# The middle stage's value products with the values as TensorE's weights, two heads in the two halves of its columns

## The reference, cut to what matters

```python
xn, ln_lat = layer_norm(ctx), layer_norm(x)          # 375 and 112 rows a batch
q = ln_lat @ Wq                                      # 16 heads x 64
k, v = split(concatenate([xn, ln_lat]) @ Wkv)        # 487 rows
weight = softmax(einsum('bhld,bhnd->bhln', q * scale, k * scale), masked)
out = einsum('bhln,bhnd->bhld', weight, v)           # 112 x 64 for each head
x = x + tanh(g) * (out.reshape(b, 112, 1024) @ Wout)
# then layer norm, and a router that picks 2 of 8 experts for each token
```

## Time and profile before

| | |
|---|---|
| median of three runs | 1403.51 us |
| the profiled execution's own time | 1406.79 us |
| its span, first to last instruction | 1405.0 us |
| mean granted TensorE clock | 0.937 |
| TensorE matmul busy | 1225.0 us, 87% |
| VectorE busy | 1083.2 us, 77% |
| ScalarE busy | 999.4 us, 71% |
| GpSimd busy | 813.3 us, 58% |

### The profile page before, as it was taken

One profiled execution on the slowest core, in us unless ns is written; L12 is line 12 of the kernel. 1 busy time (PEld: TensorE's weight loads), 2 busy tenths in 40 slices (PEclk: granted clock), 3 DMA queues, 4 the chain that ended last, 5 costly groups with the idle time before them and its releaser, 6 DMA issues. The chain is left out here.

```text
span 1405.0 us, 38066 instructions
## 1 busy us (share of the span) xinstructions
PE 1225.0 (87%) x13060; PEld 880.3 (63%) x13060; DVE 1083.2 (77%) x3112; ACT 999.4 (71%) x2552; POOL 813.3 (58%) x1204
## 2 busy tenths in 40 slices
PE   3999999999986499999999999999999974489994
PEld 1777777777764245566656566656666653389894
DVE  3799999999985168888888888888888882477872
ACT  2888888888883358877787887787888771256562
POOL 3544444444454346677777777777777674146564
PEclk7799999999987599999999999999999985699997
DMA  5444545455420148877788777878777793854333
GB/s 162 131 146 144 148 120 169 114 151 155 134 50 7 49 94 156 141 147 146 153 158 160 143 146 154 147 151 163 152 144 152 137 196 61 316 154 60 57 36 76
DMA packets 309406, 185.50 MB, mean 132 GB/s; under 512 B 257930, under 2 KB 295186, under 8 KB 306112
## 3 DMA queue, kind: packets, MB, share of 16 engines
q1 hardware_dynamic: 293024, 140.82, 47.3%
q0 software_dynamic: 13168, 35.80, 10.5%
q10 hardware_dynamic: 3024, 6.47, 1.5%
HBM read 76.19 MB, written 49.94 MB: 90 GB/s over the span
## 5 line engine op out<-in xcount | busy, mean ns | idle before, releaser
L1682 ACT ACTIVATE b_prob<-b_prob,b_top 112x487 f32<-112x487 f32 x256 | 178.9, 699 | 28.3 <-DVE b_top L1808 26.5
L1315 POOL TENSOR_TENSOR b_halves<-b_prob,b_halves 112x487 f16<-112x487 f32 x128 | 146.9, 1148 | 83.7 <-ACT b_halves L1707 82.2
L1493 PE MATMUL b_ps_p<-w_s,b_tok_s 128*128 128x512 f16 (+1 forms) x768 | 187.7, 381 | 4.0 <-DVE b_k_s L1795 3.2
L1493 PE MATMUL b_ps_p<-b_tok_s,w_s 128*128 128x487 f16 x768 | 181.9, 374 | 6.6 <-POOL b_tok_s L1309 3.7
L1808 DVE CUSTOM_DVE_ANT_0 b_prob<-b_ps_s,b_keep 112x487 f32<-112x487 f32 x256 | 167.3, 655 | 13.2 <-PE b_ps_s L1586 11.6
L717 ACT ACTIVATE a_prob<-a_prob,a_top 112x375 f32<-112x375 f32 x256 | 154.8, 605 | 3.7 <-DVE a_top L853 2.0
L1707 ACT ACTIVATE b_halves<-b_prob 112x487 f16<-112x487 f32 x256 | 156.0, 609 | 0.6
L853 DVE CUSTOM_DVE_ANT_0 a_prob<-a_ps_s,a_keep 112x375 f32<-112x375 f32 x256 | 138.1, 540 | 21.7 <-PE a_ps_s L610 21.4
L618 PE MATMUL a_ps_t<-a_const,a_prob 112*125 112x112 f32 x768 | 135.7, 287 | 10.6 <-ACT a_prob L717 9.1
L1601 PEld LDWEIGHTS b_ps_o<-b_v_s,b_pT 128*128 128x128 f16 (+1 forms) x3072 | 123.9, 99 | 31.4 <-DMA b_pT<-b_halves 11.6
L1601 PE MATMUL b_ps_o<-b_v_s,b_pT 128*128 128x64 f16 (+1 forms) x3072 | 135.0, 195 | 9.2 <-DMA b_pT<-b_halves 9.1
(11 more groups left out here) (263 smaller groups left out, 3022.9 us busy)
## 6 DMA issues: line engine op xcount, KB each, us to landing
xs<-a_blank SPq DMA_DIRECT2D x14, 1032.0 KB, 4.5
c_w_pool<-w_split SPq DMA_DIRECT2D x8, 1600.0 KB, 10.6
b_wch_f<-in_w_experts POOLq DMA_DIRECT2D x32, 384.0 KB, 5.2
w_split<-b_wch_s POOLq DMA_DIRECT2D x32, 384.0 KB, 3.9
a_k_stack<-keys SPq DMA_DIRECT2D x96, 93.8 KB, 3.1
a_ctx_f<-in_ctxT SPq DMA_DIRECT2D x16, 375.0 KB, 3.8
keys<-a_k_s SPq DMA_DIRECT2D x16, 375.0 KB, 3.2
b_ctx_t<-in_ctx SPq DMA_DIRECT2D x16, 375.0 KB
```

What stands on the lines that cost most here:

```text
L1315: pool.tensor_tensor(halves[:, h % TURN, LO, 0:NK], prob[:, h % RING, 0:NK], halves[:, h % TURN, HI, 0:NK], ALU.subtract).then_inc(s_lo[1], 1)
L1493: last = pe.matmul(out, sta(a, k), mov(m, k), start=(k == 0 and n == 0), stop=(k == tiles - 1 and n == 2))
L1682: act.activation(prob[:, h % RING, 0:NK], prob[:, h % RING, 0:NK], ACT.Exp, bias=top[:, h % RING:h % RING + 1], scale=-1.0, accum_out=sums ...
```

## The change

Values and probabilities change places in `values`. It is called once for a pair of heads, at even steps, six steps behind (`PAIRLAG`). It does 24 matmuls: weights are 64 columns of the values, moving are the 112 columns of `pT`, and the two heads alternate between output partitions 0 to 63 and 64 to 127, each with its half of the array's columns. The output thus stands in `ps_o` with the head's 64 numbers in the partitions and the tokens in the columns, as Wout's product wants it.

Since the softmax sums lie in one partition for each token, they can't scale that output directly. So the reciprocals of eight heads are turned by TensorE (`H_T`, one transpose of 112 x 8), split into high and low by VectorE (`rT`, scaled by 4096), spread over the partitions by TensorE (`H_B`, eight matmuls with weights of 8 rows, `picks`), copied to SBUF by ScalarE (`r_f`) and multiplied with `ps_o` by VectorE (`o_f`). ScalarE takes the high half of `o_f` (`out_high`), GpSimd the low half (`out_low`). `o_n`, its multiplication, the eight transposes a batch and the VectorE low half of `oT` are gone. The "h" parts of a batch are seven, not five, and lie at steps 0, 1, 5, 9, 13, 14, and the first one at step 15 of the batch itself.

```diff
-LAG = 5
+PAIRLAG = 6
-        pT = sb("pT", [128, TURN, 2, NB1, 128], F16)
+        pT = sb("pT", [128, TURN, 2, NB1, T], F16)
-        H_T, H_O, H_X, H_G, HI_ = 0, 2, 3, 4, 5
+        H_T, H_B, H_O, H_X, H_G, NH = (0, 2), (1, 3), 4, 5, 6, 7
+        FREED = (2, 3, 5, 6, 7, 8, 9)
-        XSLOT = {1: ("h", 0), 2: ("r", 0), 3: ("q", 0), 4: ("q", 1), 6: ("h", 1), 8: ("n", 0), 9: ("h", 2), 10: ("n", 1), 11: ("n", 2),
-                 13: ("h", 3), 14: ("h", 4)}
+        XSLOT = {0: ("h", H_B[0]), 1: ("h", H_T[1]), 2: ("r", 0), 3: ("q", 0), 4: ("q", 1), 5: ("h", H_B[1]), 8: ("n", 0), 9: ("h", H_O),
+                 10: ("n", 1), 11: ("n", 2), 13: ("h", H_X), 14: ("h", H_G), 15: ("t", H_T[0])}
 # GpSimd
+            def out_low(c, i):
+                need(pool, s_hhi, AH, c, A_O[i], settled)
+                pool.tensor_tensor(oT[:, LO, 4 * i:4 * i + 4, :], o_f[i][:, :].rearrange("p (j n) -> p j n", j=4), oT[:, HI, 4 * i:4 * i + 4, :],
+                                   ALU.subtract).then_inc(s_olo, 1)
 # GpSimd, body
+                        if s in (3, 7):
+                            out_low(b - 1, s // 7)
 # TensorE, hitem
-                if k < H_O:
-                    for n in range(4):
-                        j = 4 * k + n
-                        last = pe.transpose(ps_x[:, n * T:(n + 1) * T], o_n[:, 2 * j:2 * j + 2, :].rearrange("p h d -> p (h d)"), ident[0:T, 0:T])
+                if k in H_T:
+                    i = H_T.index(k)
+                    need(pe, s_rsum, 2, c, i + 1)
+                    last = pe.transpose(ps_x[0:8, 0:T], rsum[:, 8 * i:8 * i + 8], ident[0:T, 0:T])
+                elif k in H_B:
+                    for j in range(4):
+                        for part in (HI, LO):
+                            last = pe.matmul(ps_x[:, j * T:(j + 1) * T], picks[:, j, :], rT[:, part, :], start=(part == HI), stop=(part == LO))
 # TensorE, values
-                        last = pe.matmul(ps_o[h // 8][:, col:col + D1], pT[0:k, h % TURN, a, j, :],
-                                         v_s[par][0:k, m, j, h * D1:(h + 1) * D1], ...
+                        for half in range(2):
+                            h = 2 * pair + half
+                            last = pe.matmul(ps_o[pair // 4][64 * half:64 * half + 64, cols], v_s[par][0:k, m, j, h * D1:(h + 1) * D1],
+                                             pT[0:k, h % TURN, a, j, :], ...
 # ScalarE
+                if k in H_B:
+                    act.activation(r_f[:, :], ps_x[:, 0:4 * T], ACT.Copy).then_inc(s_hhi, 1)
+            def out_high(c, i):
+                act.activation(oT[:, HI, 4 * i:4 * i + 4, :], o_f[i][:, :].rearrange("p (j n) -> p j n", j=4), ACT.Copy).then_inc(s_hhi, 1)
 # VectorE
-                dve.tensor_tensor(o_n[:, heads, :], ps_o[i][0:T, :].rearrange("p (h d) -> p h d", h=8),
-                                  rsum[:, heads].unsqueeze(2).to_broadcast([T, 8, D1]), ALU.mult).then_inc(s_oread, 1)
+                if k in H_T:
+                    dve.tensor_scalar(rT[:, HI, :], ps_x[0:8, 0:T], WHOLE, None, ALU.mult).then_inc(s_hfree, 1)
+                    dve.scalar_tensor_tensor(rT[:, LO, :], ps_x[0:8, 0:T], WHOLE, rT[:, HI, :], ALU.mult, ALU.subtract).then_inc(s_hfree, 1)
+                elif k in H_B:
+                    dve.scalar_tensor_tensor(o_f[i][:, :], ps_o[i][:, 0:4 * T], 1.0 / WHOLE, r_f[:, :], ALU.mult, ALU.mult).then_inc(s_hfree, 1)
 # VectorE, body: hitem follows the step's item
-                    kind, k = XSLOT.get(s - 1, ("", 0))
+                    kind, k = XSLOT.get((s - 1) % H, ("", 0))
```

More of the change, by code:

```diff
@@ L1004 @@
 KLAST = NK - (NB1 - 1) * KB1
-LAG = 5
+PAIRLAG = 6
+WHOLE = 4096.0
 SCALE1 = D1 ** -0.5
@@ L1061, in phase_attention_large_heads @@
         halves = sb("halves", [T, TURN, 2, NB1 * KB1], F16)
-        pT = sb("pT", [128, TURN, 2, NB1, 128], F16)
+        pT = sb("pT", [128, TURN, 2, NB1, T], F16)
         x_res = sb("x_res", [T, D], F32)
         rsum = sb("rsum", [T, H], F32)
-        o_n = sb("o_n", [T, H, D1], F32)
+        picks = sb("picks", [8, 4, 128], F16)
+        rT = sb("rT", [8, 2, T], F16)
+        r_f = sb("r_f", [128, 4 * T], F32)
+        o_f = [sb(f"o_f{i}", [128, 4 * T], F32) for i in range(2)]
         oT = sb("oT", [128, 2, IT, T], F16)
@@ L1478, in _ @@
             send_rows(B - 2)
+            for i in range(2):
+                out_low(B - 1, i)
             deviation3(B - 1)
@@ L1588, in scores, with values @@
                 last.then_inc(s_score, 1)
-            def values(b, par, h):
-                need(pe, s_turned[h % RING], 16 * (H // RING), b, 16 * (h // RING + 1))
-                if h == 0:
+            def values(b, par, pair):
+                for h in (2 * pair, 2 * pair + 1):
+                    need(pe, s_turned[h % RING], 16 * (H // RING), b, 16 * (h // RING + 1))
+                if pair == 0:
                     need(pe, s_ihi, PI, b, PI)
                     need(pe, s_ifree, PI, b, PI)
-                if h % 8 == 0:
-                    need(pe, s_oread, 2, b - 1, h // 8 + 1)
-                col = (h % 8) * D1
+                if pair % 4 == 0:
+                    need(pe, s_hfree, HF, b - 1, FREED[H_B[pair // 4]])
+                cols = slice((pair % 4) * T, (pair % 4 + 1) * T)
                 for j in range(NB1):
@@ L1626, in body @@
                         lend(b, par, s)
-                    if not (first(b) and s < LAG):
-                        values(*behind(s, LAG, b, par))
+                    if s % 2 == 0 and not (first(b) and s < PAIRLAG):
+                        c, p, h = behind(s, PAIRLAG, b, par)
+                        values(c, p, h // 2)
             pe.wait_ge(s_setup, 16 * 9)
-            pe.wait_ge(s_zero, 8)
+            pe.wait_ge(s_zero, 7)
             for c, items in ((0, range(4)), (1, range(4, PI))):
@@ L1642, in _ @@
             run_batches(pe, body)
-            for h in range(H - LAG, H):
-                values(B - 1, 1, h)
-            need(pe, s_hfree, HI_, B - 1, 0)
+            need(pe, s_hfree, HF, B - 1, FREED[0])
+            hitem(B - 1, 1)
+            for pair in range((H - PAIRLAG) // 2, H // 2):
+                values(B - 1, 1, pair)
+            need(pe, s_hfree, HF, B - 1, FREED[1])
             ranks(B - 2)
             need(pe, s_rank, 1, B - 1, 0)
[L1648 to L1651, removed]
+            for k in range(2, NH):
+                need(pe, s_hfree, HF, B - 1, FREED[k - 1])
                 hitem(B - 1, k)
-            need(pe, s_hfree, HI_, B, 0)
+            need(pe, s_hfree, HF, B, 0)
             ranks(B - 1)
@@ L1734, in body @@
                         normalise(b + 2)
+                    if not first(b) and s in (2, 7):
+                        out_high(b - 1, s // 7)
                     if not (first(b) and s < 1):
@@ L1769, in _ @@
             weigh(B - 2)
-            for k in range(HI_):
+            for i in range(2):
+                hitem(B - 1, H_B[i])
+                out_high(B - 1, i)
+            for k in range(H_O, NH):
                 hitem(B - 1, k)
@@ L1887, in body @@
                             item(b + 1, 1 - par, k)
-                    kind, k = XSLOT.get(s - 1, ("", 0))
+                    kind, k = XSLOT.get((s - 1) % H, ("", 0))
                     if kind == "q" and ahead(b, 1):
                         item(b + 1, 1 - par, ITEMS.index((kind, k)))
-                    if kind == "h" and not first(b):
+                    if kind in ("h", "t") and not first(b):
                         hitem(b - 1, k)
@@ L1916, in _ @@
             run_batches(dve, body)
+            hitem(B - 1, H_T[0])
             low_half(B - 1, H - 2)
             combine_weights(B - 2)
+            shares(B - 1, 1, 1)
+            hitem(B - 1, H_B[0])
             ranks(B - 2)
-            out_heads(B - 1, 1, 1)
-            for k in range(H_X):
+            for k in range(H_T[1], H_X):
                 hitem(B - 1, k)
```

100 lines of the change are left out of this document (55 added, 45 removed).

## The result

The changed kernel takes 1473.03 us (median of 4 runs, 1470.37 to 1476.6) where the kernel before takes 1404.2 in the same comparison: ratio 1.0491, 95% interval 1.0461 to 1.0521. It is slower by 69 us; 37 were forecast. The direction held, and the time lies inside the wide range (1397 to 1482) but outside the forecast's own (1418 to 1462): the size was off by nearly a factor of two.

What follows compares the result with a forecast made beforehand. TensorE's own sequence bounds the kernel, each us a batch counting 14 times; -0.32 + 0.86 + 1.12 + 0.87 = +2.53 us a batch, 35.4 over 14, plus 1.5 at the ends: +37, 1440 us (own range 1418 to 1462, wide 1397 to 1482).

Steps and rivals of the forecast that it cites:

- Values and changes of shape: TensorE's value pairs at 55 ns a round: -0.32 us a batch; entering and leaving full array shape: +0.86.
- The other TensorE work: Eight f32 transposes replaced by two small transposes and 16 broadcast matmuls, with shape changes: net +1.12 us a batch.
- The waits: TensorE's handoff waits at step 0, the ranks and the last value item together: net +0.87 us a batch.
- The wait at step 0: TensorE's broadcast 0 stands still for VectorE's rT, behind maxima, low half and value item: 1.7 us a batch.
- The ranks' wait: TensorE's ranks wait for rT of transpose 1: 0.25 us a batch, in place of 0.87 before.
- The small wait for the last value item: Item 1's wait on TensorE, 0.21 us a batch before, is swallowed by the wait at step 0.
- Beside the path: VectorE gets a net relief; ScalarE's copies and GpSimd's subtractions fit in spare time: no us added.
- The ends: Last batch +0.5 us; tail from the last values to Wout's product +1.0 us.
- my own test: Prediction is wrong if the period, forecast at 44.3 us, is under 42.5 or over 46.
- No overlap: Column halves don't run side by side, a pair takes 1.20 us: 1504 us; with half-way cases (1468), chance 0.16.
- Free shapes: Changes of array shape cost nothing, the wait stays: +0.77 us a batch, 1415 us (1404 to 1418); chance 0.13.
- Faster: Value pairs at about 0.62 us or less, shape changes included, and short step 0 waits: 1395 us; chance 0.16.

Runs made afterwards that it cites:

- Experiment 2: Changed kernel with item 0's product computed twice, directly ahead of the wait at step 0; 12.3 us faster than the changed kernel.
- experiment 8: Kernel before the change with ScalarE's normalise split over steps 6 and 7; 1396.2 us, a gain of 8.0.
- experiment 6: Changed kernel with both rT reads (steps 0 and 2) ahead of the maxima and ScalarE's normalise split over steps 6 and 7; 1423.64 us.
- kernel 11: Kernel of experiment 6 with VectorE's statistics moved from step 3 to 4 and GpSimd's deviation from 4 to 5; 1405.7 us.
- experiment 3: Changed kernel with a pair's two loops exchanged: all twelve matmuls of one head, then all twelve of the other; 1516.7 us.
- kernel 12: Kernel of experiment 8 with VectorE's statistics moved from step 3 to 4 and GpSimd's deviation from 4 to 5; 1396.0 us.
- experiment 7: Kernel of experiment 6 with picks and rT over 128 rows, zero outside the eight that count; 1423.45 us against 1423.64.
- experiment 1: Changed kernel with VectorE's rT read at step 0 moved ahead of the maxima; 1438.55 us.
- experiment 9: Kernel of experiment 6 with VectorE's combine weights moved from step 1 to 5 and GpSimd's label from 3 to 5; slower by some 8 us.
- experiment 10: Kernel of experiment 8 with VectorE's combine weights moved from step 1 to 5 and GpSimd's label from 3 to 5; slower by some 6 us.

## Why the prediction was half right

**What bounds it.** Right: TensorE's sequence, and each us in a batch counts 14 times. The mean period is 46.06 against 41.81, +4.25 where +2.53 was forecast, and 14 times this is 59.5 of the 68.8 us.

**Values and changes of shape.** The form was right, the terms too dear. A round of two takes 49.5 ns, not 55; a load of 64 columns lasts 110 ns each in the trace but is hidden. Start to start, all value matmuls of a batch with the ways in and out took 6.38 us before and take 6.35 after: -0.03, where I had -0.32 + 0.86. Coming from a full matmul, the first value matmul starts 0.093 us later than another full one would (199 against 106 ns behind the transposes, 299 against 206 behind an item), as I assumed; but the way from the pair into the scores is hardly dearer than it was (0.14 against 0.12 us). The two halves start 3 to 5 ns apart. The Trainium skill (TensorE: Matmul & The Clock Gate, Measured speedup vs the span model) has some 4 ns for each further tile that runs along, and the trace agrees. By an estimate from its price of a load (LDWEIGHTS there, columns / 1.2 GHz, so 53 ns for 64 columns) the round would be 107 ns; the measured 49.5 ns decides against that.

**The other TensorE work.** +0.70 a batch, not +1.12: the steps around 8-row and 8-column matmuls cost 0.09 each way at most, and the two transposes cost 0.10 from start to start as assumed. Together TensorE's own work rose by 0.67 us a batch where I summed 1.66. With the waits as I forecast them that would have given 14 x (0.67 + 0.87) + 1.5 = 23 us, some 1427.

**The waits: the step that failed.** I gave them +0.87. They are +2.67 as idle time and +2.78 from start to start, which is how I had counted, and the clock behind them adds 0.82 (1.65 every second batch). Together 3.60, which with 0.67 makes 4.27; the period rose by 4.25.
- The wait at step 0 was right in place, cause and size: forecast 1.7, measured 1.86. Not foreseen: that behind an idle time of this length the clock falls, here in every second batch. Experiment 2 shows it, since more work there made the kernel 12 us faster.
- The ranks' wait: from start to start 0.66 against 0.25 forecast and 0.89 before (idle 0.50 and 0.72). The small wait for the last value item went, as forecast.
- Missing altogether, from start to start: 0.50 at the query items, 0.47 more at the first value item (0.96 against 0.49 with the next one), 0.37 more at the router. I followed VectorE through steps 0 to 2 only and read the other handoffs as if their slack were unchanged. They had little: the same normalise block cost 0.49 before (experiment 8). An explanation that fits is that single heads had stood in every step, 0.35 us of work between a product and the next that needs its bank, while a pair stands in every second one. That is argued, not shown. Shown is that these waits go when other engines' queues are reordered (experiments 6 and 11) with TensorE's order as it is.

**Beside the path.** "A net relief" for VectorE was hardly true: 300 of 400 us busy against 334, but the periods are longer, and a batch takes 34.6 us of it against 34.9. It also said nothing, since at five places TensorE waited for VectorE. GpSimd's low halves (1.03 us each) came up in no wait of TensorE in the steady state.

**The ends.** Last batch +1.0 (forecast 0.5), tail +1.0 (forecast 1.0).

**The rivals.** No overlap: the trace and experiment 3 refute it. Free shapes: nearer for TensorE's work (-0.10 against the measured +0.67 and my +1.66), wrong for the time. Faster: its condition, a pair of 0.62 us, came out as 0.72 + 0.09, and its short wait didn't come. A slower case by clock was not among them. By my own test, the period of 46.06 lies just past the upper limit of 46.

**What the change is worth.** With queues reordered on both sides, kernel 11 takes 1405.7 us and kernel 12 takes 1396.0: the change as a whole (value products, transposes, broadcasts) costs 9.7 us, against 68.8 in the first comparison. Of these, 12 periods of 0.28 are 3.4; most of the rest lies in the last batch and its tail. In the middle the handoffs cost 0.92 us a batch from start to start against 1.25, and TensorE's work without them is 40.68 against 40.07. That is +0.61, about the +0.67 of the first comparison. So 59 of the 69 us went by reordering alone, with the new products as they are. Reordering more of either kernel was not tried.

## What to carry to other kernels

When a change moves a producer or a read, follow every engine's queue through the whole period, not only around the new wait: one wait removed here became the next one (1.87 us, then 1.4 at the ranks, then 1.4 at the query items) until the operation that truly stood ahead, 1.8 us of statistics, was moved. Put small reads that TensorE waits for ahead of large operations whose own data is not there yet. Before a restructured kernel is judged, give both versions the same care with their queues. Price a wait of TensorE by the starts on both sides of it and not by the idle time alone (0.49 us against 0.20 here), and with the clock that follows it.

## What the runs showed of the hardware

- Matmuls of 128 rows by 64 columns in the two halves of the columns, alternating, run two in 49.5 ns with 112 columns moving: the price of one. With the halves in turn, each takes 49 ns.
- One idle time of 1.87 us in a batch whose other ones were 0.80 us or less was followed, in every second batch, by some 3 us at a granted clock of 0.50; with 0.63 us in its place (experiment 2) the clock stayed at 1.00. In experiment 1 waits of 1.4 us left it at 1.00 too.
- Full 128-row weights for the broadcasts in place of 8-row ones made the steps into them 96 ns shorter (206 against 302 ns, experiment 7).
- One and the same VectorE subtraction of 112 x 487 numbers took between 0.65 and 2.34 us, depending on where it stood (experiments 6, 9 and 10).
